# First feed-forward weight matrix quantised early and held as int8, with reordered feed-forward steps and rounding in one step

## The reference, cut to what matters

```python
def act_quant(x):
    scale = 127.0 / jnp.clip(jnp.max(jnp.abs(x), axis=-1, keepdims=True), 1e-05)
    q = jnp.clip(jnp.round(x * scale), -128.0, 127.0) / scale
    return x + jax.lax.stop_gradient(q - x)

def weight_quant(w):
    scale = 1.0 / jnp.clip(jnp.mean(jnp.abs(w)), 1e-05)
    q = jnp.clip(jnp.round(w * scale), -1.0, 1.0) / scale
    return w + jax.lax.stop_gradient(q - w)

def bitlinear(x, w, b):
    return jnp.einsum('bsd,fd->bsf', act_quant(rmsnorm(x)), weight_quant(w)) + b

h = jax.nn.gelu(bitlinear(x, w1, b1), approximate=False)
return bitlinear(h, w2, b2)
```

## Time and profile before

| | us |
|---|---|
| median of 3 runs | 803.56 |
| lowest and highest run | 803.52, 804.91 |
| the profiled execution's own time | 805.4 |
| its span in the trace | 803.7 |
| PE busy in the span | 777.5 (97%) |
| DVE busy | 586.9 (73%) |
| ACT busy | 387.0 (48%) |
| POOL busy | 48.7 (6%) |

### The profile page before, as it was taken

How to read it: one execution, slowest core, us unless ns; L and a number is a source line. 1 busy time by engine, 2 the same in 40 slices (tenths; PEclk the granted TensorE clock), 3 DMA queues, 4 the chain that set the end, 5 groups by cost and what they waited for, 6 DMA issues and landing times. The chain is left out here.

```text
span 803.7 us, 11529 instructions
## 1 busy us (share of the span) xinstructions
PE 777.5 (97%) x4270; PEld 687.8 (86%) x4270; DVE 586.9 (73%) x1240; ACT 387.0 (48%) x800; POOL 48.7 (6%) x88
## 2 busy tenths in 40 slices
PE   5999999999999899999998799999999999999998
PEld 5888878889999899998876488888888879999886
DVE  8988888645554788998689968889896677675331
ACT  5222123444443576775676647574673343454220
POOL 3000000000000000101102211000002020000000
PEclk9999999999999999999999999999999999999999
DMA  5522124432334322319965349234135135334331
GB/s 188 184 80 79 53 70 141 130 114 97 116 121 150 100 73 73 118 29 332 270 235 144 104 117 279 91 105 157 53 107 144 55 121 146 130 132 154 122 130 39
DMA packets 28775, 102.17 MB, mean 127 GB/s; under 512 B 3736, under 2 KB 3864, under 8 KB 28464
## 3 DMA queue, kind: packets, MB, share of 16 engines
q1 hardware_dynamic: 24784, 86.76, 32.1%
q0 software_dynamic: 3936, 14.68, 8.3%
HBM read 91.99 MB, written 1.57 MB: 116 GB/s over the span
## 5 line engine op out<-in xcount | busy, mean ns | idle before, releaser
L1197 DVE TENSOR_TENSOR w_lo<-raw,w_hi 128x1024 fp32r<-128x1024 f32 x140 | 169.7, 1221 | 64.9 <-ACT w_hi L907 64.5
L907 ACT ACTIVATE w_hi<-raw 128x1024 fp32r<-128x1024 f32 x140 | 147.3, 1057 | 105.9 <-PE bank L1983 79.6
L1931 PE MATMUL bank<-xn1T,w_hi 128*128 128x384 f32 x416 | 106.8, 337 | 0.0
L1983 PE MATMUL bank<-w_hi,xn3T 128*128 128x512 f32 x288 | 92.1, 393 | 0.0
L1931 PEld LDWEIGHTS bank<-xn1T,w_hi 128*128 128x128 f32 x416 | 74.3, 188 | 0.9 <-issue 0.3
L1931 PE MATMUL bank<-xn1T,w_lo 128*128 128x384 f32 x208 | 69.6, 335 | 0.0
L1983 PEld LDWEIGHTS bank<-w_hi,xn3T 128*128 128x128 f32 x288 | 54.1, 188 | 11.0
L1931 PE MATMUL bank<-xn4T,w_hi 128*128 128x384 f32 x240 | 61.2, 335 | 0.0
L1983 PE MATMUL bank<-w_lo,xn3T 128*128 128x512 f32 x144 | 56.0, 389 | 0.0
L1931 PEld LDWEIGHTS bank<-xn4T,w_hi 128*128 128x128 f32 x240 | 43.2, 188 | 0.0
L1931 PE MATMUL bank<-xn4T,w_lo 128*128 128x384 f32 x120 | 40.2, 335 | 0.0
(11 more groups left out here) (363 smaller groups left out, 1717.2 us busy)
## 6 DMA issues: line engine op xcount, KB each, us to landing
raw<-weights SPq DMA_DIRECT2D x140, 512.0 KB, 3.3
row_sb<-rows SPq DMA_DIRECT2D x6, 512.0 KB, 5.9
kcat<-kcat POOLq DMA_DIRECT2D x16, 192.0 KB, 2.8
base<-rows POOLq DMA_DIRECT2D x6, 512.0 KB, 13.2
w2r<-w_in SPq DMA_DIRECT2D x1, 2048.0 KB, 9.8
w1r<-w_in POOLq DMA_DIRECT2D x1, 2048.0 KB, 9.2
x_sb<-x_in SPq DMA_DIRECT2D x3, 512.0 KB, 4.6
row_sb<-rows SPq DMA_DIRECT2D x6, 256.0 KB, 4.8
```

Source lines behind the costliest of these rows:

```text
L907: act.activation(w_hi[:, u % RING], raw[:, u % RAW], ACT.Copy).then_inc(hi_split, 1)
L1197: dve.tensor_tensor(w_lo[:, u % RING], raw[:, u % RAW], f(w_hi[:, u % RING]), ALU.subtract).then_inc(unit_split, 1)
L1931: last = pe.matmul(out_of(pr)[:, 0:N], w[pa][:, slot, k * P:(k + 1) * P], TT[src][:, pb, k], start=(k == 0 and m == 0), stop=(k == KD - 1 ...
L1983: last = pe.matmul(out_of(pr)[:], tile[:, pa, k, ts], w[pb][:, at_, j * HALF:(j + 1) * HALF], start=(kk == 0 and j == 0 and m == 0 and nam ...
```

## The change

It does four things. (1) w1 is loaded from SP's queue after unit k1.2, once mixo.3 is done, into the region AT, and goes through `ffn_abs`, `ffn_mean` and `w_cast` among the units k1.3 to k1.7; `w_cast` writes it as 8-bit integers into row slot 0 (`w1_small`). (2) A new ACT step `w_open` after wo.5 turns the integers into the bf16 `w1q` once the last head is done. The load of wg0, which shares row slot 0, waits for it. (3) The steps of the feed-forward block stand in another order. (4) in_round and h_round are one DVE operation each, without the clip, which can change nothing where the factor is 127 over the row's own maximum. The diff, with most unchanged lines left out:

```diff
@@ -126,7 +126,13 @@
     steps.append(("mix0_out", (2, 3)))
-    run("k1", 1, 8)
+    run("k1", 1, 4)
+    steps.append(("ffn_abs", 0))
+    run("k1", 4, 5)
+    steps.append(("ffn_mean", 0))
+    run("k1", 5, 7)
+    steps.append(("w_cast", 0))
+    run("k1", 7, 8)
     unit("k2", 0)
@@ -162,31 +168,33 @@
     steps.append(("ffn_mean", 1))
-    run("wo", 5, 7)
+    run("wo", 5, 6)
+    steps.append(("w_open",))
+    run("wo", 6, 7)
     steps.append(("w_cast", 1))
-    steps.append(("ffn_abs", 0))
     run("wo", 7, 12)
-    steps.append(("ffn_mean", 0))
...
-    steps.extend([tiled("wo", 1, 0), ("gelu_table",), tiled("wo", 1, 1), ("in_stats", 0), ("w_cast", 0), ("in_amax", 0),
-                  tiled("wo", 1, 2, 0, 2), ("in_factor", 0), ("in_stats", 1), ("in_scale", 0), ("in_round", 0),
-                  tiled("wo", 1, 2, 2, 4), ("ahead_hi",), ("in_amax", 1), ("ahead_hi",), ("in_factor", 1), ("in_T", 0),
-                  ("in_stats", 2), ("in_scale", 1), ("in_ev", 0), ("in_amax", 2), ("ahead_hi",), ("ffn_h", 0),
-                  ("in_factor", 2), ("in_round", 1), ("in_scale", 2), ("in_round", 2), ("in_T", 1), ("hn", 0), ("in_ev", 1),
-                  ("in_T", 2), ("ahead_lo",), ("gelu", 0), ("ffn_h", 1), ("square", 0), ("h_max", 0), ("in_ev", 2),
-                  ("h_factor", 0), ("h_round", 0), ("ffn_h", 2), ("hn", 1), ("h_cast", 0), ("ahead_lo",),
-                  ("gelu", 1), ("square", 1), ("h_max", 1), ("h_T", 0), ("hn", 2), ("h_ev", 0), ("ahead_hi",), ("h_factor", 1), ("gelu", 2),
-                  ("h_round", 1), ("ffn_o", 0), ("square", 2), ("h_max", 2), ("h_cast", 1), ("h_factor", 2), ("h_round", 2),
-                  ("h_T", 1), ("h_cast", 2), ("x_out", 0), ("h_ev", 1), ("h_T", 2), ("ffn_o", 1), ("h_ev", 2), ("ffn_o", 2),
-                  ("x_out", 1), ("x_norm", 0), ("xn3_T", 0), ("ahead_lo",), ("xn3_hi", 0), ("x_norm", 1),
-                  ("xn3_lo", 0), ("ahead_lo",), ("x_out", 2)])
+    steps.extend([tiled("wo", 1, 0), ("gelu_table",), tiled("wo", 1, 1), ("in_stats", 0),
+                  ("in_amax", 0), ("in_factor", 0), ("in_scale", 0), ("in_round", 0), tiled("wo", 1, 2, 0, 2),
+                  ("in_stats", 1), ("ahead_hi",), ("in_amax", 1), tiled("wo", 1, 2, 2, 4), ("in_factor", 1),
+                  ("ahead_lo",), ("in_scale", 1), ("in_round", 1), ("in_T", 0), ("in_stats", 2), ("in_T", 1),
+                  ("in_ev", 0), ("in_ev", 1), ("ffn_h", 0), ("in_amax", 2), ("in_factor", 2), ("ffn_h", 1),
+                  ("in_scale", 2), ("hn", 0), ("gelu", 0), ("in_round", 2), ("square", 0), ("in_T", 2), ("h_max", 0),
+                  ("in_ev", 2), ("hn", 1), ("h_factor", 0), ("gelu", 1), ("ffn_h", 2), ("h_round", 0), ("h_max", 1),
+                  ("h_cast", 0), ("square", 1), ("h_T", 0), ("hn", 2), ("h_ev", 0), ("h_factor", 1), ("gelu", 2),
+                  ("ffn_o", 0), ("h_round", 1), ("square", 2), ("h_max", 2), ("h_cast", 1), ("h_factor", 2),
+                  ("h_round", 2), ("h_T", 1), ("x_out", 0), ("h_cast", 2), ("h_ev", 1), ("h_T", 2), ("ahead_hi",),
+                  ("ffn_o", 1), ("h_ev", 2), ("x_out", 1), ("ffn_o", 2)])
     run("g1", 0, 4)
-    steps.extend([tiled("g1", 0, 0, 0, 2), ("xn3_T", 1), ("xn3_hi", 1), ("xn3_lo", 1), tiled("g1", 0, 0, 2, 4), ("x_norm", 2),
-                  tiled("g1", 0, 1, 0, 2), ("xn3_T", 2), ("xn3_hi", 2), ("xn3_lo", 2), tiled("g1", 0, 1, 2, 4), ("g1_out", 0),
-                  tiled("g1", 0, 2, 0, 2), tiled("g1", 0, 2, 2, 4), ("g1_out", 1), ("ahead",), ("ahead",), ("g1_out", 2)])
+    steps.extend([("x_norm", 0), ("ahead_hi",), ("xn3_T", 0),
+                  ("ahead_lo",), ("xn3_hi", 0), ("xn3_lo", 0), tiled("g1", 0, 0, 0, 2), ("ahead_hi",), ("ahead_lo",),
+                  ("x_norm", 1), ("ahead_lo",), ("xn3_T", 1), ("x_out", 2), tiled("g1", 0, 0, 2, 4), ("xn3_hi", 1),
+                  ("xn3_lo", 1), tiled("g1", 0, 1, 0, 2), ("x_norm", 2), ("xn3_T", 2), tiled("g1", 0, 1, 2, 4),
+                  ("xn3_hi", 2), ("xn3_lo", 2), ("g1_out", 0), tiled("g1", 0, 2, 0, 2), tiled("g1", 0, 2, 2, 4),
+                  ("g1_out", 1), ("ahead",), ("ahead",), ("g1_out", 2)])
@@ -493,7 +501,9 @@
         base2 = at("base2", [P, NT, D], F32, R1 + 12)
-        w1r = at("w1r", [P, KD * HID], F32, R2)
+        w1r = at("w1r", [P, KD * HID], F32, AT + 14)
+        w1_abs = at("w1_abs", [P, KD * HID], BF16, AT + 6)
+        w1_small = at("w1_small", [P, KD * HID], mybir.dt.int8, ROWS_AT)
         w2r = at("w2r", [P, KH * D], F32, R3)
@@ -612,6 +622,7 @@
         w_abs, w_unit, w_quant = sem("w_abs"), sem("w_unit"), sem("w_quant")
+        w1_kept = sem("w1_kept")
         sq_ready, rms_ready = sem("sq_ready"), sem("rms_ready")
@@ -720,12 +731,16 @@
                             load_row(n)
+                    if (name, i) == ("k1", 2):
...
+                        wait_full(sp, "mixo.3")
+                        sp.dma_start(w1r[:], w1_in).then_inc(ffn_landed[0], 16)
                     if (name, i) == ("wo", 1):
...
                     if (name, i) == ("g1", 1):
-                        load_row("wg0", lambda: wait_emptied(sp, "v2.1.2"))
+                        load_row("wg0", lambda: sp.wait_ge(w_quant, 1))
                     if (name, i) == ("wo", 8):
@@ -854,8 +869,6 @@
                         add_row("mix_bo", t, base1).then_inc(base1_ready, 16)
-                    wait_full(pool, "attend.15")
-                    pool.dma_start(w1r[:], w1_in).then_inc(ffn_landed[0], 16)
                 if s == ("g1_out", NT - 1):
@@ -1061,17 +1074,24 @@
                     act.wait_ge(ffn_landed[w], 16)
-                    src, dst = ((w1r, w1q), (w2r, w2q))[w]
-                    act.activation(dst[:].rearrange("p a b -> p (a b)"), src[:], ACT.Abs,
+                    src, dst = ((w1r, w1_abs[:]), (w2r, w2q[:].rearrange("p a b -> p (a b)")))[w]
+                    act.activation(dst, src[:], ACT.Abs,
                                    accum_out=w_s[:, 0, w:w + 1]).then_inc(w_abs, 1)
...
                     w = s[1]
-                    src, dst = ((w1r, w1q), (w2r, w2q))[w]
-                    act.wait_ge(w_unit, 2 - w)
+                    act.wait_ge(w_unit, w + 1)
                     act.wait_ge(consts, 7)
-                    act.activation(dst[:].rearrange("p a b -> p (a b)"), src[:], ACT.Identity,
-                                   bias=minus_round[:]).then_inc(w_quant, 1)
+                    if w == 0:
+                        wait_emptied(act, "v2.1.2")
+                        act.activation(w1_small[:], w1r[:], ACT.Identity, bias=minus_round[:]).then_inc(w1_kept, 1)
+                    else:
+                        act.activation(w2q[:].rearrange("p a b -> p (a b)"), w2r[:], ACT.Identity,
+                                       bias=minus_round[:]).then_inc(w_quant, 1)
+                if kind == "w_open":
+                    wait_full(act, f"attend.{H0 - 1}")
+                    act.wait_ge(w1_kept, 1)
+                    act.activation(w1q[:].rearrange("p a b -> p (a b)"), w1_small[:], ACT.Copy).then_inc(w_quant, 1)
                 if kind == "gelu_table":
@@ -1611,8 +1631,7 @@
                     dve.wait_ge(in_nat, t + 1)
-                    link(dve.tensor_scalar(xn2[:, t], xn2[:, t], ROUND, ROUND + 127.0, ALU.add, ALU.min))
-                    dve.tensor_scalar(xq[:, t], xn2[:, t], ROUND - 128.0, ROUND, ALU.max, ALU.subtract).then_inc(in_quant, 1)
+                    dve.tensor_scalar(xq[:, t], xn2[:, t], ROUND, ROUND, ALU.add, ALU.subtract).then_inc(in_quant, 1)
                     dve.wait_ge(in_power, t + 1)
@@ -1634,8 +1653,7 @@
                     dve.wait_ge(sq_ready, t + 1)
-                    link(dve.tensor_scalar(hn[:, t], hn[:, t], h_s[:, 5, t:t + 1], ROUND, ALU.mult, ALU.add))
-                    dve.tensor_scalar(hn[:, t], hn[:, t], ROUND + 127.0, ROUND - 128.0, ALU.min, ALU.max).then_inc(h_rounded, 1)
+                    dve.tensor_scalar(hn[:, t], hn[:, t], h_s[:, 5, t:t + 1], ROUND, ALU.mult, ALU.add).then_inc(h_rounded, 1)
                 if kind == "x_out":
@@ -2046,7 +2064,7 @@
                     w = s[1]
-                    pe.wait_ge(w_abs, 2 - w)
+                    pe.wait_ge(w_abs, w + 1)
                     wait_bank(pe, f"w_sum.{w}")
@@ -2104,7 +2122,7 @@
                     if t == 0:
-                        pe.wait_ge(w_quant, 2)
+                        pe.wait_ge(w_quant, 1)
                     wait_bank(pe, pr)
@@ -2120,6 +2138,8 @@
                     t = s[1]
+                    if t == 0:
+                        pe.wait_ge(w_quant, 2)
                     wait_emptied(pe, f"hqT.{t}")
```

## The result

Slower by 0.3%. The changed kernel takes 807.18 us (median of 8 runs, 803.14 to 807.89) where the kernel before, measured beside it, takes 805.00 (8 runs, 803.26 to 805.85): ratio 1.003, 95% interval 1.0017 to 1.0043. The forecast was 803.6 and its range ended at 807.0. The profiled execution took 807.1, 1.7 more than that of before (805.4).

The account below looks back on a forecast made before the run. PE, busy 97% of the span, was taken as the bound. Terms -5.4 (feed-forward block), +3.3 (stall), +1.7 (clock) and +0.4 (steps among k1) gave 0.0; with the median 1.8 under the profile's 805.4, 803.6 us, range 801.0 to 807.0.

Parts of the forecast that it names:

- Part 3, the clock: At k1.3, after PE's idle wait: a lower granted clock loses 1.7 us, bounds 0 and 2.
- The sum: All terms add to 0.0, leaving the profiled 805.4; the runs' median, 1.8 lower, was kept: 803.6 us.
- the feed-forward block: From wo.7 to the end of g1: 5.4 us gained, all told.
- sum product and wait: Among k1, behind k1.4: w1's sum product waits 0.26 and costs 0.14, 0.4 us lost.
- the stall: Before k1.3: its load comes behind w1's 2 MB on SP's queue, 3.3 us lost, bounds 2.0 and 7.6.
- 3 x 0.87: In the feed-forward block: an entry for transposes in the 13.3 us of products between PE's waits.
- Part 2: Feed-forward block, new order and one-step rounding: first ffn_h at 434.45 instead of 436.16, g1 starting 5.7 us earlier.
- Part 1: Quantisation of w1 leaves the feed-forward block: 1.0 us gained; int8 operand between 0.3 us less and twice the time.
- B: Rival at k1: w1 and the unit behind land late, stall 7.6 instead of 3.3, 807.9 us; chance 0.12.
- C: Rival in the feed-forward block: new order leaves more holes, 3 us at the hand-overs, 806.5 us; chance 0.15.
- D: Rival at k1: the clock holds, 801.9 us, or 801 with a slightly quicker load; chance 0.20.
- E: Rival at k1: the load is hidden if k1.3 is not held behind w1, 798.6 us; chance 0.08.

Follow-up runs that it names:

- experiment 9: Changed kernel with 8 unneeded products put on PE before k1.3: 804.96 us, ratio 1.0015 to the kernel before.
- experiment 6: Kernel before with SP's wait for mixo.3 after k1.2's load and no transfer behind it: 803.58 us, ratio 0.9993.
- experiment 8: Kernel before with 12 unneeded products on PE before the first product of attention 0: 803.92 us, ratio 0.9993.
- experiment 1: Changed kernel with w1's load and SP's wait hung on unit k1.6 instead of k1.2: 800.83 us, ratio 0.9956 to the kernel before.
- experiment 10: Changed kernel with w1's load and the wait for mixo.3 moved from SP's queue to POOL's: 800.94 us, ratio 0.9947 to the kernel before.
- experiment 2: Changed kernel with 16 unneeded products put on PE before k1.3: 805.81 us, ratio 1.0017 to the kernel before.
- experiment 3: Changed kernel with w1's load hung on unit k1.3 instead of k1.2: 802.04 us, ratio 0.9974 to the kernel before.
- experiment 5: Kernel of experiment 1 with the feed-forward steps in the order of before, without w1's old w_cast: 801.74 us, ratio 0.9968 to the kernel before.
- experiment 4: Kernel before with only in_round and h_round made one DVE operation each: 802.95 us, ratio 0.9983.

## Why the prediction was wrong

The path was right step by step, and the result lies 3.6 above the forecast (807.2 against 803.6). Two steps failed, and their errors were of one sign.

- **Part 3, the clock: "3.3 us of full idleness just after dense work is worse, so I count 1.7; bounds 0 and 2".** This term was mis-sized, and its upper bound too. It measured 2.9 in the stretch table and 2.7 against experiment 9. The sentence said that the case is worse than the earlier trace rows and then took its number. The low stretch lasted 6.8 us here after 3.00 idle us (3.4 in the earlier trace rows), and there was none in the two profiles with 1.52 and 1.55. Each microsecond at half clock costs half a microsecond. An upper end from the rows would have been k1.3 wholly at half clock, 4.2 us. This is 1.2 of the 3.6. None of the rivals was a clock dearer than the earlier trace rows, so the range had no end for it.
- **The sum: "The median of the runs is 1.8 lower, and I keep that".** The profiled execution of before took 805.4 and the three runs had a median of 803.56. Over eight runs that median is 805.00: its runs fall in two clumps, 803.3 to 803.6 and 804.9 to 805.9, and two of the three lay in the lower one, the profile in the upper. The changed kernel's profile (807.1) and median (807.18) agree, so the discount was wrong in full: 1.9 of the 3.6. Which three runs were drawn was chance; that a median of three can lie in either clump was not priced. On a base of 805.0 the same sum of nothing would have said 805.0.
- **The remaining 0.5** is small terms: the feed-forward block 5.1 instead of 5.4, sum product and wait 0.5 instead of 0.4, the stall 3.16 instead of 3.3, and the 0.2 between k2.0 and wo.7.

Two figures of the working don't come out of their own terms, and neither moves the forecast: the lower bound of 2.0 for the stall (437 GB/s from 1.0 us after the issue gives 1.2), and the transposes "3 x 0.87" in the 13.3 of products, which counts one of them.

What was right: SP silent from 202.6 to 221.65 (measured 202.59 to 221.67), w1 landing after 7.7 (7.6), k1.3's split at 230.7 (230.59), PE's start at 233.1 (232.96), and from wo.7 to the end of g1 not 61 but 55.6 (55.9, from 422.30 + 0.39). The Trainium skill's bandwidth rule (DMA: Bandwidth & Descriptors, section Bandwidth) would have made the stall 3.6; the trace gives 3.16 and sides with the rate of the earlier trace rows, with 401 GB/s while PE stood. Part 2 was walked over thirty hand-overs and came out within 0.3; the waits it named are the ones in the timeline: 0.65, 0.65, 1.21, 0.73, 0.62, 0.66 and 0.42 for in_ev 0, the third xq, in_ev 2, h_ev 0, h_cast 2, x_norm 0 and xn3_hi 0. The int8 operand, in no row before, costs nothing: 3.70 us for the cast, where the cast to bf16 took 3.71, and 3.60 for w_open, as long as the nearest row. Part 1's "twice the time" was far off.

One reservation on the 5.1. It compares two profiles, and in that of before the clock fell in the block: the 16 products of ffn_o took 5.09, now 3.63. Experiment 6, whose steps in the block are those of before, kept its clock there (3.63 for the same 16 products), and the distance from wo.7 to the end of g1 is 60.75 us, the same as in experiment 8:

```profile
414.34 0.39 PE L1985 MATMUL bank<-w_hi,mixoT 128*128 128x512 f32 x1
...
475.09 12.24 PE bank L1985 x54
```

So 0.6 of the 5.1 is clock (the products themselves took 1.5 longer, but experiment 6 has a wait of 0.65 before the next transposes that before doesn't have), and the change itself takes 4.5 off the block: 1.5 by the order and 3.0 by the rounding and by w1 leaving. The timed kernels agree. Experiments 1 and 10 have the whole gain and only the price of the sum product, 4.5 - 0.6 = 3.9, and are 3.2 and 4.0 under before by the medians (3.5 and 4.3 by the ratios).

Of the rivals, B (the unit lands late) did not decide: the stall was smaller than forecast, not 1.6 larger. C (more holes) did not come either. D (the clock holds) is at most one run in eight: the changed kernel's fastest, 803.14, is its only one with a mean granted clock of 1.00, and there is no trace of it. E said that the load is hidden if the unit isn't held behind it. On one queue it is held; on two it isn't, and then the load is hidden: experiment 10 (800.9) is E's 798.6, plus the 1.4 by which the base was off, plus 0.9 of gain that the block did not give (4.5 for 5.4). The cause of the stall is settled by experiments 1, 6 and 10: SP's wait puts 2 MB ahead of a unit on one queue, and PE gets that unit 3.2 us late. That the idleness costs nearly as much again in clock rests on the profiles of the changed kernel and of experiments 2 and 9, and on the mean clocks of the runs. Left open are the spread of experiment 9, what decides whether the clock falls, and the 0.2 between k2.0 and wo.7.

## What to carry to other kernels

A transfer that waits for a product must not stand on the queue that feeds the critical engine's next operands: give it to another queue, or hang it where the units behind have slack; that alone turned +0.3% into -0.5% here. When TensorE runs without a pause, price a new hole of some 3 us at up to twice its length, since the clock after it can take as much again (3.2 and 2.9 us here). And take the base from many runs: here a median of three with a profile 0.2% above it was a sign of two clumps, not a discount.

## What the runs showed of the hardware that I had not expected

- The granted clock after a hole is partly chance. The hole of 2.19 us in front of attention 0 is in every kernel that has no filler there, to the hundredth. In the stretch from 266 to 290 the clock was 0.93 in the profiles of before, after and experiments 1, 2, 3 and 5 (0.07 x 24 = 1.7 us lost), and 1.00 in those of 4, 6, 9 and 10. Which of the two comes is not settled by the steps of the kernel, for in the block after the attention it goes the same way: experiments 1 and 10 have the same steps there, and the clock held in one profile and fell in the other. The kernel before and experiment 6 do the same work there at the same time (the hole ends at 272.81 and 272.88); the same stretch, first of before and then of experiment 6:

```profile
266.00:290.00 24.00, 21.35 (x117) 20.25 (x116) 17.43 (x36) 15.31 (x31) 1.03 (x2) 0.93 0.28 87
```

```profile
266.00:290.00 24.00, 21.35 (x130) 20.22 (x129) 18.95 (x40) 16.51 (x34) 2.06 (x4) 1.00 0.34 107
```

- The spread of the runs goes with it. The 73 runs of before that stood beside the experiments have medians of 803.3 to 803.5 where the mean granted clock was 0.999 or 1.000 (25 runs) and 804.9 to 805.6 where it was 0.998 or less (48 runs): 1.5 us, about one stretch at half clock. It is no strict rule: nine of the 48 took less than 804.
- A second queue made no transfer quicker. With w1 on POOL's queue, w1 took 8.5 us and the two unit loads issued meanwhile 6.1 and 4.8 (experiment 10). With w1 and the units on SP's queue at nearly the same times, w1 took 7.5 and they took 5.2 and 4.6 (experiment 1). Alone a unit takes 3.2. What the other queue gives is that SP doesn't have to wait.
